# Twelve of sixteen batches rolled into a run-time loop, in two of the four layers of a graph network

## The chip, the core and the metric

The kernel runs on one core of a Trainium2 chip. The metric is the device time of one execution in microseconds. Before the change the median of three runs is 2392.07 us (2391.06 to 2393.24).

## What is computed

The input is x, 16 batches of 1024 nodes with 64 features, and an adjacency matrix of 1024 x 1024. Four attention layers follow each other; each one is added to its input and normed over the features:

```python
x = _layernorm(x + _L0_gnn_ref(x, L0_gnn_W, L0_gnn_a, adj))      # additive attention
x = _layernorm(x + _L1_gnn_ref(x, w0, b0, wa, ba, adj))          # softmax per feature
x = _layernorm(x + _L2_gnn_ref(x, adj, L2_gnn_W, L2_gnn_a))      # additive attention
x = _layernorm(x + _L3_gnn_ref(x, adj, Wh, bh, Wo, bo, g, b))    # dot-product attention
```

The second layer weighs the features of the neighbours, feature by feature:

```python
feat = softplus(x * (INV_SQRT2 * w0) + b0)
scores = feat * wa + ba
attn = softmax(where(mask, scores, -1e9), over neighbours)
out = einsum('bijd,bjd->bid', attn, feat)
```

The fourth layer has four heads and a second attention over their projection. Each attention scores every node against every other, masks, and mixes:

```python
def _gat_layer(h, mask, b):
    scores = einsum('...nd,...md->...nm', h, h)
    attn = softmax(where(mask, scores, NEG), axis=-1)
    return einsum('...nm,...md->...nd', attn, h) + b
h = einsum('bnc,hdc->bhnd', x, Wh)
z = leaky_relu(concatenated heads of _gat_layer(h, mask, bh))
h2 = einsum('bnk,dk->bnd', z, Wo)
z2 = leaky_relu(_gat_layer(h2, mask, bo))      # then layernorm with gamma, beta
```

## The kernel before

x stays in SBUF for all 16 batches (`keep.x`), and so does the mask. The program has a set-up and four stages, one per layer, with a barrier between them. In each stage every engine has its own instruction list, written by hand, and the engines meet only through semaphores that count up over the batches. A wait for "batch b" is a wait for a count such as `HEADS * b + 2`. `wait(engine, semaphore, count)` at L32 emits one, and leaves it out where the count is a number of zero or less.

The order on each engine is the order in which the Python code is run. `additive_layer` (first and third layer) steps over the batches in a Python loop of its own. `feature_layer` (second layer) has a `step(b, s)` for each engine, with `s` the parity of b for the double buffers; each step works on batch b and prepares b + 1 and b + 2. TensorE's step turns the maxima of a tile (L1781), spreads the maximum over the partitions (L1787), sums up the features (L1795) and multiplies mask and weighted features in four banks (L1809, L1813). DVE's step reduces the maximum (L1637, L1640), shifts, splits values into a rounded part and the rest (L1654) and divides. POOL adds the residual (L1592), and DVE takes its sums (L102).

`dot_layer` (fourth layer) cuts a batch into twenty steps: eight for the first head pair ("s0" to "s7"), eight for the second ("r0" to "r7"), and four ("e0" to "e3") for the second attention of the batch before. In each step TensorE computes scores (L1327, L1330, L1333, or L1351 to L1360 for the second attention) into PSUM, ACT takes the exponential (L1175, L1182) into one of four weight buffers, DVE multiplies by the mask (L1027, L1034), and TensorE multiplies with the values (L1375, L1389) one step later. Between scores and product TensorE does the small jobs that the table in `jobs` assigns to the step: the picking of denominators (L1288), the heads (L1295), the projection (L1303) and others. `Before(st)` gives the step whose product follows a step's scores, also over the border of a batch. SP swaps halves of the second attention's operands (L818, L822) and stores a finished batch (L827); it already does so in a run-time loop, `sp.Fori(0, BATCH - 1)`, in both versions.

The change touches the two functions called `run_all`. Before it, each is a Python loop over 16 batches, so that every instruction stands in the program 16 times with its counts as plain numbers:

```python
for b in range(BATCH):
    run_batch(run, b, b % 2, first=b == 0, last=b == BATCH - 1)
```

## Time and profile before

| | us |
|---|---|
| median of three runs | 2392.07 |
| profiled execution, its own time | 2392.07 |
| its span | 2390.3 |
| TensorE (matmul) busy | 2096.2 (88%) |
| DVE busy | 1791.1 (75%) |
| ACT busy | 1321.2 (55%) |
| POOL busy | 720.5 (30%) |

A row of the timeline reads: start in us, duration in us, engine, line, operation, what is written and read, how many records in a row, and in brackets the idle time before it with the engine that ended it. PE is TensorE's matmul, PEld its weight load, SPq the DMA issue of SP. One fp32 matmul call leaves two records of matmul and two of weight load. Register and branch instructions are not shown as rows.

### The profile page before, as it was taken

The numbers are of one execution on the slowest core, as the hardware profiler recorded it, in microseconds if no ns is written. First come the engines' busy times: TensorE is split into PE (matmuls) and PEld (weight loads), VectorE is DVE, ScalarE is ACT, GpSimd is POOL, SyncE is SP. The second block draws the span as 40 slices with busy tenths as digits, with TensorE's granted clock in tenths as the row PEclk, the third lists the DMA queues.
The fourth block names the chain that finished last, engine by engine and source line by source line (L and its number), as shares of the span: only waits on it lengthen the run. The fifth ranks groups of instructions, "written<-read, shape, count | busy, mean of one in ns | idle before, by whom it ended". The sixth has DMA issues, their size and how long they took to land.

```text
span 2390.3 us, 52998 instructions
## 1 busy us (share of the span) xinstructions
PE 2096.2 (88%) x22580; PEld 1379.1 (58%) x22580; DVE 1791.1 (75%) x2182; ACT 1321.2 (55%) x2970; POOL 720.5 (30%) x527
## 2 busy tenths in 40 slices
PE   6888828886788865999999999999999999999993
PEld 5676727776566653555655555555555555654552
DVE  5788838888688875668688788778777778778773
ACT  3576754442376763556466566565566565566552
POOL 1334325665344330003123123123123123123124
PEclk8788969999798986999999999999999999999996
DMA  5000000000000000000000000000000000000000
GB/s 142 2 2 2 2 2 1 1 1 1 2 2 2 3 2 5 1 10 10 5 15 10 6 15 10 6 14 10 6 14 10 6 15 13 2 14 14 2 14 19
DMA packets 30778, 24.69 MB, mean 10 GB/s; under 512 B 21776, under 2 KB 25424, under 8 KB 30544
## 3 DMA queue, kind: packets, MB, share of 16 engines
q1 hardware_dynamic: 30544, 21.31, 3.7%
q8 instruction: 178, 2.92, 0.5%
q14 instruction: 56, 0.46, 0.1%
HBM read 8.72 MB, written 4.19 MB: 5 GB/s over the span
## 4 chain that ended last, share of the span: by engine, by line
PE 58%; DVE 2%; POOL 1%; SPq 0%; ACT 0%; issue 0%; DMA 0%; ACTq 0%; POOLq 0%; DVEq 0%
PE fourth_ps_out L1375 20%; PE fourth_ps_scores L1327 7%; PE fourth_ps_out L1389 5%; PE fourth_ps_scores L1330 5%; PE fourth_ps_scores L1333 5%; PE fourth_ps_prep L1295 3%; PE fourth_ps_prep L1303 3%; PE fourth_ps_prep L1288 3%; PE fourth_ps_scores L1351 2%; PE fourth_ps_scores L1354 1%; PE fourth_ps_scores L1357 1%; PE fourth_ps_scores L1360 1%; PE fourth_ps_prep L1278 1%; PE fourth_ps_prep L1256 1%; DVE fourth_weights L1027 1%; PE fourth_ps_prep L1310 0%
## 5 line engine op out<-in xcount | busy, mean ns | idle before, releaser
L1027 DVE TENSOR_TENSOR fourth_weights<-fourth_weights,keep_mask 128x1024 f32<-128x1024 f32 x512 | 681.3, 1369 | 217.3 <-ACT fourth_weights L1175 215.7
L1175 ACT ACTIVATE fourth_weights<-fourth_ps_scores 128x512 f32<-128x512 f32 x1024 | 529.3, 606 | 422.7 <-PE fourth_ps_scores L1333 422.7
L1375 PE MATMUL fourth_ps_out<-fourth_weights,fourth_x_stage 128*64 128x512 f32 x2048 | 496.5, 605 | 0.0
L1375 PEld LDWEIGHTS fourth_ps_out<-fourth_weights,fourth_x_stage 128*64 128x64 f32 x2048 | 122.9, 136 | 232.6 <-issue 197.5
L1327 PE MATMUL fourth_ps_scores<-fourth_g_high,fourth_x_high 64*128 64x512 f32 x1024 | 230.3, 446 | 2.4 <-DVE fourth_g_low L986 2.4
L1327 PEld LDWEIGHTS fourth_ps_scores<-fourth_g_high,fourth_x_high 64*128 64x128 f32 x1024 | 96.6, 184 | 200.4 <-issue 105.5
L1182 ACT ACTIVATE fourth_weights<-fourth_ps_scores 128x1024 f32<-128x1024 f32 x128 | 125.3, 1025 | 143.0 <-PE fourth_ps_scores L1360 138.0
L634 PE MATMUL first_ps_out<-first_values,first_weights 128*64 128x65 f32 x4096 | 165.3, 244 | 44.0 <-issue 32.1
L1333 PE MATMUL fourth_ps_scores<-fourth_g_low,fourth_x_high 64*128 64x512 f32 x1024 | 203.2, 392 | 0.0
L1330 PE MATMUL fourth_ps_scores<-fourth_g_high,fourth_x_low 64*128 64x512 f32 x1024 | 203.1, 392 | 0.0
L1034 DVE TENSOR_TENSOR fourth_weights<-fourth_weights,keep_mask 128x1024 f32<-128x1024 f32 x128 | 153.0, 1236 | 66.5 <-ACT fourth_weights L1182 66.4
L634 PE MATMUL third_ps_out<-third_values,third_weights 128*64 128x65 f32 x4096 | 162.2, 241 | 44.4 <-issue 32.3
L634 PEld LDWEIGHTS first_ps_out<-first_values,first_weights 128*64 128x64 f32 x4096 | 150.5, 157 | 72.0 <-issue 53.3
L634 PEld LDWEIGHTS third_ps_out<-third_values,third_weights 128*64 128x64 f32 x4096 | 146.6, 153 | 70.8 <-issue 48.7
L431 DVE SCALAR_TENSOR_TENSOR third_weights<-third_row,third_gain,keep_mask 128x1024 f32<-128x1024 f32 x128 | 168.3, 1336 | 10.0 <-ACT third_row L529 9.5
L431 DVE SCALAR_TENSOR_TENSOR first_weights<-first_row,first_gain,keep_mask 128x1024 f32<-128x1024 f32 x128 | 165.7, 1316 | 9.9 <-ACT first_row L529 9.4
L1809 PE MATMUL second_ps_out<-second_parts,keep_mask 128*128 128x256 f32 x1024 | 155.3, 301 | 0.0
L1809 PEld LDWEIGHTS second_ps_out<-second_parts,keep_mask 128*128 128x128 f32 x1024 | 141.1, 204 | 5.6 <-issue 2.7
L1389 PEld LDWEIGHTS fourth_ps_out<-fourth_h_values,fourth_weights 128*64 128x64 f32 x4096 | 124.6, 138 | 18.9 <-issue 17.5
L1389 PE MATMUL fourth_ps_out<-fourth_h_values,fourth_weights 128*64 128x65 f32 x4096 | 133.3, 223 | 1.1 <-DVE fourth_weights L1034 1.1
L881 POOL TENSOR_TENSOR fourth_biased<-fourth_mixed,fourth_rows_in 128x512 f32<-128x512 f32 x16 | 33.1, 2066 | 325.1 <-DVE fourth_mixed L1042 325.1
L1333 PEld LDWEIGHTS fourth_ps_scores<-fourth_g_low,fourth_x_high 64*128 64x128 f32 x1024 | 97.4, 185 | 22.5
(263 smaller groups left out, 3455.4 us busy)
## 6 DMA issues: line engine op xcount, KB each, us to landing
setup_adj<-in_adj SPq DMA_DIRECT2D x8, 512.0 KB, 6.4
fourth_h_high<-fourth_h_high SPq DMA_DIRECT2D x32, 128.0 KB, 2.3
fourth_h_low<-fourth_h_low SPq DMA_DIRECT2D x32, 128.0 KB, 2.3
out<-keep_x SPq DMA_DIRECT2D x16, 256.0 KB, 2.6
keep_x<-in_x SPq DMA_DIRECT2D x1, 512.0 KB, 10.9
fourth_bias_rows<-in_L_gnn_bh SPq DMA_DIRECT2D x8, 0.2 KB
fourth_wh_in<-in_L_gnn_Wh SPq DMA_DIRECT2D x2, 32.0 KB
fourth_wo_in<-in_L_gnn_Wo SPq DMA_DIRECT2D x1, 64.0 KB
```

The source lines that it names most:

```text
L431: dve.scalar_tensor_tensor(out=weights[t % RING][:, :], in0=row[s][:, :], scalar=gain[s][:, t:t + 1], in1=keep.mask[:, t, :].bitcast(F32), ...
L634: last = pe.matmul(ps_out[part, i * WIDE:i * WIDE + AUG], weights[t % RING][:, i * P + c * SIDE:i * P + (c + 1) * SIDE], values[s][:, t, 0 ...
L1027: dve.tensor_tensor(buf[:, :], buf[:, :], keep.mask[:, st.t, :].bitcast(F32), ALU.mult)\
L1034: dve.tensor_tensor(buf[:, :], buf[:, :], keep.mask[:, 2 * p + u, :].bitcast(F32), ALU.mult)\
L1175: act.activation(weights[st.slot + g][:, cols(half)], ps_scores[g][:, cols(half)], ACT.Exp)\
L1182: act.activation(weights[slot + u][:, :], ps_scores[u][:, :], ACT.Exp).then_inc(exp_ready, 2)
L1327: pe.matmul(ps_scores[g][:, cols(half)], x_high[s][rows(g), nodes], g_high[pair][rows(g), cols(half)], start=True, stop=False)
L1330: pe.matmul(ps_scores[g][:, cols(half)], x_low[s][rows(g), nodes], g_high[pair][rows(g), cols(half)], start=False, stop=False)
L1333: last = pe.matmul(ps_scores[g][:, cols(half)], x_high[s][rows(g), nodes], g_low[pair][rows(g), cols(half)], start=False, stop=True)
L1375: last = pe.matmul(ps_out[rows(half), cols(g)], x_stage[st.s][:, st.t, half, :], weights[st.slot + g][:, cols(half)], start=(st.t == 0), s ...
L1389: last = pe.matmul(ps_out[c * SIDE:(c + 1) * SIDE, i * WIDE:i * WIDE + AUG], weights[slot + u][:, i * P + c * SIDE:i * P + (c + 1) * SIDE] ...
L1809: pe.matmul(out, keep.mask[:, t, i * P:(i + 1) * P], parts[s][:, t, :, :].rearrange("p s c -> p (s c)"), start=(t == 0), stop=False, skip_ ...
```

## The change

In the second and the fourth layer the batches are divided anew. In the fourth layer batches 0, 1, 14 and 15 stay written out, and batches 2 to 13 become a run-time loop with six passes of two batches. In the second layer steps 0, 13, 14 and 15 stay written out, and steps 1 to 12 become the loop. Each engine but SP gets a loop of its own; no barrier is added. Inside the loop b is an expression of the loop register, so the counts of waits and the addresses `keep.x[:, b]` are computed at run time.

```diff
-        def run_all(run):
-            for b in range(BATCH):
-                run_batch(run, b, b % 2, first=b == 0, last=b == BATCH - 1)
+        def run_all(engine, run):
+            run_batch(run, 0, 0, first=True)
+            run_batch(run, 1, 1)
+            with engine.Fori(0, (BATCH - 4) // 2) as i:
+                run_batch(run, 2 * i + 2, 0)
+                run_batch(run, 2 * i + 3, 1)
+            run_batch(run, BATCH - 2, 0)
+            run_batch(run, BATCH - 1, 1, last=True)
...
-                run_all(run)
+                run_all(pool, run)
...
-                run_all(run)
+                run_all(dve, run)
...
-                run_all(run)
+                run_all(act, run)
...
-                run_all(run)
+                run_all(pe, run)
...
-        def run_all(step):
...
-            for b in range(BATCH):
+        def run_all(engine, step):
...
+            step(0, 0)
+            with engine.Fori(0, (BATCH - 4) // 2) as i:
+                step(2 * i + 1, 1)
+                step(2 * i + 2, 0)
+            for b in range(BATCH - 3, BATCH):
                 step(b, b % 2)
...
         def has(b):
...
-            return 0 <= b < BATCH
+            return not isinstance(b, int) or 0 <= b < BATCH
...
-                run_all(step)
+                run_all(pool, step)
...
-                run_all(step)
+                run_all(dve, step)
...
-                run_all(step)
+                run_all(act, step)
...
-                run_all(step)
+                run_all(pe, step)
```

How the lists change is seen best at three places. The names in brackets are semaphores that an instruction waits for; a semaphore number that an earlier stage has used is shown under that stage's name (in the fourth layer `first_low_ready` and `first_total_ready` are the ones for the two score operands). ISA and REGISTER_ALU are register instructions of the engine's sequencer.

TensorE, fourth layer, the border between two batches before the change: the last product of the step before, then the scores of the next batch.

```order
L1360 MATMUL fourth_ps_scores<-fourth_h_norm,fourth_ones 128x512 x2
L1389 MATMUL fourth_ps_out<-fourth_h_values,fourth_weights 64x65 [waits fourth_weights_ready]
L1389 MATMUL fourth_ps_out<-fourth_h_values,fourth_weights 64x65 x15
L1389 MATMUL fourth_ps_out<-fourth_h_values,fourth_weights 64x65 [waits fourth_weights_ready]
L1389 MATMUL fourth_ps_out<-fourth_h_values,fourth_weights 64x65 x15
L1327 MATMUL fourth_ps_scores<-fourth_g_high,fourth_x_high 128x512 [waits fourth_exp_ready,first_low_ready,first_total_ready]
L1327 MATMUL fourth_ps_scores<-fourth_g_high,fourth_x_high 128x512
```

The product, two halves of sixteen matmuls, is followed directly by the scores. After the change the end of the loop body on TensorE reads:

```order
L1365 MATMUL fourth_ps_scores<-fourth_h_norm,fourth_ones 128x512 x2
L1391 ISA
L1394 MATMUL fourth_ps_out<-fourth_h_values,fourth_weights 64x65 [waits fourth_weights_ready]
L1394 MATMUL fourth_ps_out<-fourth_h_values,fourth_weights 64x65 x15
L1391 REGISTER_ALU
L1394 MATMUL fourth_ps_out<-fourth_h_values,fourth_weights 64x65 [waits fourth_weights_ready]
L1394 MATMUL fourth_ps_out<-fourth_h_values,fourth_weights 64x65 x15
L794 REGISTER_ALU
L794 COMPARE_AND_BRANCH
```

Between the product and the next scores stand the counter's increment and the branch back. The branch goes to the head of the body, where two register instructions with waits of their own now precede the scores:

```order
L794 UNCONDITIONAL_BRANCH
L794 ISA
L1327 ISA [waits first_total_ready]
L32 ISA [waits first_low_ready]
L1332 MATMUL fourth_ps_scores<-fourth_g_high,fourth_x_high 128x512 [waits fourth_exp_ready]
L1332 MATMUL fourth_ps_scores<-fourth_g_high,fourth_x_high 128x512
```

The two waits moved from the first matmul of the scores to the register instructions ahead of it. ACT, fourth layer, the exponentials of one step before the change:

```order
L1175 ACTIVATE fourth_weights<-fourth_ps_scores 128x512 [waits fourth_weights_used,fourth_scores_full]
L1175 ACTIVATE fourth_weights<-fourth_ps_scores 128x512 [waits fourth_weights_used]
L1175 ACTIVATE fourth_weights<-fourth_ps_scores 128x512 [waits fourth_scores_full]
L1175 ACTIVATE fourth_weights<-fourth_ps_scores 128x512
```

and the same step in the loop:

```order
L1176 ISA
L32 REGISTER_ALU [waits fourth_scores_full]
L1180 ACTIVATE fourth_weights<-fourth_ps_scores 128x512 [waits fourth_weights_used]
L32 REGISTER_ALU
L1180 ACTIVATE fourth_weights<-fourth_ps_scores 128x512 [waits fourth_weights_used]
L1176 REGISTER_ALU
L1180 ACTIVATE fourth_weights<-fourth_ps_scores 128x512 [waits fourth_scores_full]
L1180 ACTIVATE fourth_weights<-fourth_ps_scores 128x512
```

The wait for the scores moved from the first exponential to a register instruction in front of it, and four register instructions stand between the exponentials. The order of the matmuls, exponentials and masks themselves is the same as before everywhere. POOL, second layer, the residual in the loop:

```order
L1600 REGISTER_ALU [waits first_above_ready]
L1601 ISA [waits first_weights_used]
L1601 TENSOR_TENSOR second_norm_y<-second_mixed,keep_x 128x512
L109 TENSOR_TENSOR second_norm_centred<-second_norm_y,second_norm_minus_mean 128x512 [waits setup_loaded2]
```

Both waits of the residual stand on register instructions there; written out, they stand on the TENSOR_TENSOR.

## Rows read from the trace of the kernel before

**Rows 1.** Busy time by stretch: one batch of layer four, layer two, all of layer four.
```profile
core 0: us, PE busy (x) PEld busy (x) DVE busy (x) ACT busy (x) POOL busy (x), PEclk, DMA share, GB/s
1211.55:1300.30 88.75, 88.00 (x743) 49.98 (x743) 68.34 (x69) 51.29 (x91) 22.16 (x15) 1.00 0.04 10
400.00:580.00 180.00, 142.49 (x1091) 131.60 (x1091) 160.74 (x263) 73.55 (x149) 107.37 (x82) 0.91 0.00 1
907.00:2390.30 1483.30, 1419.28 (x11870) 806.86 (x11870) 1096.44 (x1125) 821.79 (x1440) 347.15 (x224) 0.98 0.04 10
```

**Rows 2.** TensorE's waits from 1300 to 1655 us (us in total, times, longest).
```profile
PE fourth_ps_prep L1295 <- DVE fourth_head_recip L991: 3.0, 4, 0.8
```

**Rows 3.** Second layer: its matmuls, waits from 400 to 580 us, two timeline rows.
```profile
L1809 PE MATMUL second_ps_out<-second_parts,keep_mask x1024: 277/281/582, 355.9 to 588.7; 128*128 128x256 f32 x171
...
PE second_ps_wide L1787 <- DVE second_top_wide L1640: 30.5, 12, 2.9
...
DVE second_parts L1654 <- ACT second_parts L1737: 14.5, 12, 1.8
...
494.28 1.26 POOL L1592 TENSOR_TENSOR second_norm_y<-second_mixed,keep_x 128x512 f32<-128x512 f32 x1 [1.94 <-DVE second_mixed L1667]
495.61 0.67 DVE L102 TENSOR_REDUCE second_norm_sums<-second_norm_y 128x8 f32<-128x512 f32 x1
```

**Rows 4.** The page: counts of the engines, instruction queues (packets, MB, share).
```profile
PE 2096.2 (88%) x22580; PEld 1379.1 (58%) x22580; DVE 1791.1 (75%) x2182; ACT 1321.2 (55%) x2970; POOL 720.5 (30%) x527
...
q8 instruction: 178, 2.92, 0.5%
q14 instruction: 56, 0.46, 0.1%
```

**Rows 5.** DMA issues: KB of each, median us from issue to landing.
```profile
first_w<-in_L_gnn_W SPq DMA_DIRECT2D x2, 16.0 KB, 2.0
second_factor_row<-in_L_gnn_wa SPq DMA_DIRECT2D x1, 32.0 KB, 3.2
```

**Rows 6.** Timeline of TensorE at a border between two batches of layer four.
```profile
1257.33 2.09 PE L1389 MATMUL fourth_ps_out<-fourth_h_values,fourth_weights 128*64 128x65 f32 x64
1259.34 0.50 PE L1327 MATMUL fourth_ps_scores<-fourth_g_high,fourth_x_high 64*128 64x512 f32 x2
...
1262.80 2.09 PE L1389 MATMUL fourth_ps_out<-fourth_h_values,fourth_weights 128*64 128x65 f32 x64
```

**Rows 7.** Timeline of DVE, then of ACT, at the same border.
```profile
1257.62 2.36 DVE L1034 TENSOR_TENSOR fourth_weights<-fourth_weights,keep_mask 128x1024 f32<-128x1024 f32 x2 [1.23 <-ACT fourth_weights L1182]
1261.95 1.23 DVE L1027 TENSOR_TENSOR fourth_weights<-fourth_weights,keep_mask 128x1024 f32<-128x1024 f32 x1 [1.98 <-ACT fourth_weights L1175]
1264.93 0.21 DVE L1040 RECIPROCAL fourth_recip<-fourth_ps_out 128x8 f32<-128x8 f32 x1 [1.76 <-PE fourth_ps_out L1389]
...
1260.34 2.06 ACT L1175 ACTIVATE fourth_weights<-fourth_ps_scores 128x512 f32<-128x512 f32 x4 [1.83 <-PE fourth_ps_scores L1333]
```

**Rows 8.** Timeline of POOL and SP: a store in SP's loop, the last one behind it.
```profile
1141.10 1.04 POOL L906 TENSOR_TENSOR keep_x<-fourth_outer_centred,fourth_outer_rstd 128x512 f32<-128x512 f32 x1
1142.35 0.46 SPq L827 DMA_DIRECT2D out<-keep_x  x1
...
2384.71 1.04 POOL L906 TENSOR_TENSOR keep_x<-fourth_outer_centred,fourth_outer_rstd 128x512 f32<-128x512 f32 x1
...
2385.77 0.40 SPq L827 DMA_DIRECT2D out<-keep_x  x1
```

**Rows 9.** Timeline of layer four, 1299 to 1311 us: DVE, TensorE and ACT.
```profile
1299.66 2.33 DVE L1027 TENSOR_TENSOR fourth_weights<-fourth_weights,keep_mask 128x1024 f32<-128x1024 f32 x1
...
1305.68 2.36 DVE L1027 TENSOR_TENSOR fourth_weights<-fourth_weights,keep_mask 128x1024 f32<-128x1024 f32 x2 [0.34 <-ACT fourth_weights L1175]
...
1301.13 2.00 PE L1375 MATMUL fourth_ps_out<-fourth_weights,fourth_x_stage 128*64 128x512 f32 x8
...
1309.12 1.94 PE L1375 MATMUL fourth_ps_out<-fourth_weights,fourth_x_stage 128*64 128x512 f32 x8
...
1308.55 2.06 ACT L1175 ACTIVATE fourth_weights<-fourth_ps_scores 128x512 f32<-128x512 f32 x4 [1.43 <-PE fourth_ps_scores L1333]
```

## The prediction, made before the changed kernel was run

> **What bounds the kernel now.** I read the busy shares by stretch first, then the waits of TensorE, then the timeline at the places that the change touches. The fourth layer takes the largest share of the time: it runs from 907 us to the end, 1483 of 2390.3 us [rows 1]. In its steady part one batch takes 88.75 us and TensorE is busy for 88.00 of them, at the full granted clock [rows 1]. Over four batches TensorE waits for one thing only, DVE's reciprocals of the head sums, 3.0 us in 4 waits [rows 2]. So in this layer time is added exactly when TensorE is made to stand still, and none can be taken away that is not in those 0.75 us per batch. The second layer's main matmuls (L1809) run from 355.9 to 588.7 us [rows 3]. There TensorE is busy for 142.49 of 180 us and DVE for 160.74 [rows 1]; the waits go round from TensorE over DVE and ACT, with 30.5 us of TensorE waiting for the maximum (L1787) in 12 waits, and 14.5 us of DVE waiting for ACT's rounded products [rows 3]. It is bound by a chain over engines in which DVE is almost full, and TensorE has about 2.5 us of slack in each batch. The first and third layers and the set-up are not touched.
>
> **What changes.** No arithmetic, no wait on another engine and no order of work is changed. In both layers twelve of the sixteen batches become six passes through one loop over two batches, on four engines. That adds three things: a branch back, five times per layer and engine; register work that computes each semaphore's target and the addresses of x; and, on some of those register instructions, waits that formerly sat on the matmul or activation itself. It removes instruction traffic: the whole program's was 178 packets on TensorE's queue (2.92 MB, 16.4 KB each) and 56 on the other (0.46 MB, 8.2 KB) [rows 4]. That traffic costs nothing now: in the steady fourth layer no wait of TensorE is left that it could explain [rows 2]. I therefore give its removal 0 us.
>
> **Term A, the branches back of TensorE in the fourth layer.** 22580 matmuls and as many weight loads [rows 4] came in 178 packets, 254 instructions each. One batch has 743 matmuls [rows 1], so the loop body has 2 x 2 x 743 = 2972 of these instructions, 11.7 packets long, beside the register work. Its first packet was fetched 177 us before the branch returns to it. No row shows a jump over such a distance, so I bound it. The fetch of 16 KB should cost what a 16 KB load costs from issue to landing, 2.0 us, or at most what one of 32 KB costs, 3.2 us [rows 5]. I take 2.6. Against that stands what TensorE still has queued when its sequencer meets the branch. The last piece ahead of it is the 64 records of L1389, 2.09 us; right behind it the scores of the next batch (L1327) begin [rows 6]. How many of these are already queued the trace does not say, so the cover is between 0 and 2.0 us; I take half, 1.0. The stall is then 1.6 us, with ends 0 and 3.2, and the term is 5 x 1.6 = 8.0 us, with ends 0 and 16.
>
> The packets show that instructions are brought in pieces of 16.4 and 8.2 KB [rows 4]. The Trainium skill (Runtime: NRT & Kernel Launch, "Instruction fetch mechanics") says that a taken branch whose target is outside the two pages at hand stalls until the page is fetched, and speaks against run-time loops; here it puts the stall at every one of the fourth layer's returns, as I take it, and at those of the second layer too, where it would be 8 us more if nothing hid it. Its page Advanced Engine Details and Errata ("Engine Queue Depths") gives TensorE a queue of 64 instructions; an estimate from that page would cover 64 of the 128 instructions of that 2.09 us piece, 1.0 us. No row here shows either directly.
>
> ACT, DVE and POOL branch back too, with smaller bodies. At this place they have room: DVE has the masks of the last step finished at 1259.98 while TensorE uses them from 1262.80, then idles 1.98 and 1.76 us; ACT idles 1.83 us [rows 7]. A stall of 2.6 us on them fits into the 2.8 us between mask and use, so I add 0.
>
> **Term B, waits that moved onto register instructions.** An instruction that carries its own wait starts at once; a register instruction that carries it makes the sequencer stop, and what follows is sent only afterwards. The SP queue shows the price, since it has a loop already: inside the loop the store of a batch starts 0.21 us after POOL's write of x ends (1141.10 + 1.04 to 1142.35); the last store, behind the loop and with a plain wait, starts 0.02 us after it (2384.71 + 1.04 to 2385.77) [rows 8]. So 0.19 us where the wait is the last to end, and nothing where it has long been met. In ACT's loop body the first exponential of each step now sits behind such a wait. In most steps this is hidden. In ordinary steps the second mask ends 1.0 us or more before its matmul: at 1305.68 DVE's pair takes 2.36 us and TensorE reads it from 1309.12 on [rows 9]. Two places per batch have no such room. One is the first step of the second head pair: DVE's mask runs from 1299.66 for 2.33 us, to 1301.99, inside the 2.00 us of TensorE's L1375 from 1301.13 [rows 9], whose second half needs it. The other is the reciprocal of the head sums, where TensorE waits already [rows 2]. Twelve looped batches x 2 x 0.19 = 4.6 us; ends 0 and, with twice the price at each place, 9.
>
> **Term C, the second layer.** TensorE's body there is 1.4 packets long (12 batches in 180 us are 1091 x 2 instructions, so two batches are 364), so its start may still be at hand; if it is not, 1.6 us of stall falls into the 2.5 us that TensorE waits for DVE in every batch [rows 3]. I cost the returns at 0; without that cover they would be 8 us. POOL's residual stands behind two register instructions with waits, and DVE's sums for the norm follow it; they begin 0.07 us after the residual ends, 494.28 + 1.26 to 495.61 [rows 3]. I add one 0.19 us per looped batch, 2.3 us, with ends 0 and 5.
>
> **Sum.** 8.0 + 4.6 + 2.3 = 14.9 us. The profiled execution took 2392.07 us for a span of 2390.3, 1.8 us around it, and is itself the median of the runs. So 2392.1 + 14.9 = 2407 us, 0.6% slower.
>
> **Rivals.**
> 1. The returns are covered: no more than the queued work is needed to fetch the target, or it is at hand. For it: in the steady part TensorE never waits for instructions [rows 2], so fetching runs well ahead; the piece queued at the return is 2.09 us long, about what the cheaper fetch takes. Against it: a body of 11.7 packets would have to be kept whole, or the whole piece be queued. Then A is 0 and only part of B and C is left: 2392.1 + 3 = 2395 us, no change that can be measured. This is the case on the other side, not slower than before. It decides from the point where fetching takes less than the queued 2.0 us.
> 2. Every step pays. The steady layer has twenty steps in a batch. If the register waits on ACT and TensorE ate the room in all of them, 12 x 20 x 0.19 = 46 us come on top, 2438 plus A, 2446 us. Against it: ACT idles 1.43 us before the exponentials of an ordinary step [rows 9], and a delay of 0.19 fits. A partial form, a third of the steps, is 2415 to 2425 us.
> 3. The returns cost more than one fetch: the next piece is late as well, or DVE and ACT come back so late that TensorE waits again for masks, 2 x 3.2 us per return. Five returns give 32 us, with B and C 39: 2431 us. For it: all four engines branch within one step of each other. Against it: the room in rows 7.
> 4. It becomes faster. The only stock is what the straight-line program loses to its own instruction supply. In the second layer that is part of DVE's and TensorE's small gaps, and 0 in the steady fourth. Twelve batches of the second layer at an assumed 0.25 us each give 3 us, twice that at most: 2386 to 2389 us.
>
> **How the numbers follow.** My forecast, 2399 to 2417 us, has a chance of 0.43; rival 1 has 0.25; rival 2 in its full or partial form 0.14; rival 3 0.13; rival 4 0.05. A difference under 0.2% (4.8 us) can't be told from none. Of rival 1 some 0.20 lies within that bound and 0.05 above it, of rival 4 0.02 within it. Slower by over 0.2% is then 0.43 + 0.05 + 0.14 + 0.13 = 0.75, within 0.22, faster 0.03. The range of 2391 to 2434 us leaves out the full form of rival 2, the top of rival 3 and most of rival 4. The likeliest case alone is 2399 to 2417.
>
> **What would show it.** For A: in the fourth layer five gaps of TensorE of 1 to 3 us ahead of the scores at L1327's successor, one in each second batch between the third and the fourteenth, 2 x 88.75 = 177.5 us plus the gap apart, put down to no other engine; six passes take 6 x 177.5 us plus about 13 us. For B: looped batches take about 0.4 us longer than written-out ones even without a return. For the packets: TensorE's queue still moves about as many as before in time, since the loop is fetched again in each pass; if it moves only about a third, the body was kept and rival 1 holds. For C: the second layer's stretch grows by less than 5 us, and TensorE's wait at the maximum shrinks where a return lies. I am wrong if TensorE's idle time in the steady fourth layer stays at 0.75 us per batch, or if it grows evenly over all steps; and wrong in the sum if the second layer grows by more than 8 us.

## The result and the profile after

The changed kernel takes 2446.69 us (median of 4 runs, 2444.24 to 2451.93), the kernel before 2391.74 us beside it (4 runs, 2391.06 to 2393.24). The ratio is 1.0232, with a 95% interval of 1.0211 to 1.0252: 55 us slower. The forecast was 2407 us with a range to 2434. The direction was right, the size was not, and the time lies outside the range. The profiled execution took 2449.49 us for a span of 2447.7.

The first reading is where the 57.4 us of span went. The view of one line gives the first and last start of a group (count, shortest/middle/longest duration in ns, first to last start in us):

```profile
L634 PE MATMUL third_ps_out<-third_values,third_weights x4096: 219/222/371, 615.7 to 891.3; 128*64 128x65 f32 x196
L1818 PE MATMUL second_ps_out<-second_parts,keep_mask x1024: 277/281/583, 351.8 to 585.0; 128*128 128x256 f32 x171
L1332 PE MATMUL fourth_ps_scores<-fourth_g_high,fourth_x_high x1024: 383/492/793, 934.9 to 2358.1; 64*128 64x512 f32 x171
```

In the kernel before, the rows of the third and the fourth layer read:

```profile
L634 PE MATMUL third_ps_out<-third_values,third_weights x4096: 219/222/371, 619.3 to 885.0; 128*64 128x65 f32 x196
L1327 PE MATMUL fourth_ps_scores<-fourth_g_high,fourth_x_high x1024: 383/492/793, 928.7 to 2301.2; 64*128 64x512 f32 x171
```

The looped second layer takes 233.2 us, before 232.8 [rows 3]. The fourth takes 1423.2 us, and before it took 1372.5: 50.7 us more. The third layer, in which nothing was changed, takes 275.6 us and took 265.7; the first took 4 us less than before. What of these two belongs to the change is a question for the experiments.

Busy time by stretch, with the same columns as [rows 1]:

```profile
400.00:580.00 180.00, 145.24 (x1112) 134.43 (x1113) 160.11 (x261) 73.79 (x148) 108.35 (x82) 0.91 0.00 0
...
1088.90:1177.60 88.70, 87.95 (x743) 49.90 (x741) 68.60 (x68) 51.24 (x90) 22.07 (x14) 1.00 0.05 10
1257.00:1270.10 13.10, 8.81 (x164) 6.97 (x164) 7.30 (x7) 4.82 (x5) 0.00 (x0) 0.93 0.02 5
...
1300.00:1345.00 45.00, 45.00 (x267) 22.70 (x268) 38.16 (x39) 29.90 (x57) 14.06 (x9) 1.00 0.08 18
```

The granted clock is the third number from the end. A looped batch without a return in it (1088.9 to 1177.6) takes 88.70 us, against 88.75 for a written-out one [rows 1]. So the register instructions and the waits on them cost nothing that can be seen. All of the layer's loss is at the five returns. TensorE's waits from 1000 to 2230 us (us in total, times, longest), and its timeline at the first return:

```profile
PE fourth_ps_scores L1332 <- issue: 21.5, 5, 4.5
PE fourth_ps_prep L1300 <- DVE fourth_head_recip L996: 8.1, 13, 0.8
PE fourth_ps_scores L1335 <- issue: 1.3, 3, 0.5
```

```profile
1263.65 2.09 PE L1394 MATMUL fourth_ps_out<-fourth_h_values,fourth_weights 128*64 128x65 f32 x64
1270.03 0.79 PE L1332 MATMUL fourth_ps_scores<-fourth_g_high,fourth_x_high 64*128 64x512 f32 x2 [4.29 <-issue]
```

Five standstills of 4.0 to 4.5 us, with no engine named as releaser: the first matmul after the return has not arrived. The loop's own line shows why (ns, shortest/middle/longest of six; the sixth branch is the one that leaves the loop):

```profile
L794 ACTq COMPARE_BRANCH  x6: 40/45/45, 1264.0 to 2202.1; - x6
...
L794 DVEq COMPARE_BRANCH  x6: 50/56/72, 1265.0 to 2203.2; - x6
L794 PEldq COMPARE_BRANCH  x6: 82/4478/4642, 1265.1 to 2203.2; - x6
```

TensorE's branch takes 4.3 to 4.6 us when it goes back and 0.08 us when it leaves the loop. It is met at 1265.1 us, when only 0.63 us of the last queued piece (to 1265.74) is left. In the 5.1 us from 1265 us on, two packets came over TensorE's instruction queue:

```profile
q8 instruction: 2, 0.03, 4.0%
q14 instruction: 1, 0.01, 0.4%
```

The second part of the loss begins in the gap, 1.7 us before its end (1.5 to 2.2 us before it at the five returns). The granted clock falls to its half level, 1.2 GHz, and stays there when the matmuls go on. Busy time after the first return:

```profile
1268.40:1282.10 13.70, 11.54 (x96) 9.67 (x98) 1.80 (x3) 2.17 (x4) 0.00 (x0) 0.51 0.01 2
1282.10:1296.00 13.90, 13.41 (x80) 6.74 (x76) 11.50 (x13) 7.39 (x14) 4.15 (x2) 1.00 0.01 2
```

The same 13.7 us at half clock come with each of the five returns. In the timeline above, the pair of scores lasts 0.79 us where it lasts 0.50 at full clock [rows 6]. The account for the fourth layer is then 21.5 us of standing and 29.2 us of slow matmuls, 5.8 us per return (1.3 us of the 29.2 are short gaps at L1335 between the slow matmuls). Of the 55 us between the medians, 4 are then outside the fourth layer.

In the second layer TensorE's branch back costs almost nothing:

```profile
L1552 PEldq COMPARE_BRANCH  x6: 76/210/246, 391.5 to 544.3; - x6
```

The body of 1.4 packets is at hand. From 360 to 550 us TensorE's queue moved 2 packets, before 9. Over the whole program it moved 188, before 178 [rows 4]: what the second layer saves, the refetches of the fourth more than use up.

### The profile page after: what moved, and what is told of

It is laid out like the page before. It is cut to its first block, busy times and chain, and to the rows that moved or that the text cites. A ratio compares the mean times of both kernels' runs of the same rounds, so it can differ in the third digit from the quotient of the medians.

```text
span 2447.7 us, 55658 instructions
## 1 busy us (share of the span) xinstructions
PE 2134.4 (87%) x22580; PEld 1408.4 (58%) x22580; DVE 1790.1 (73%) x2182; ACT 1321.1 (54%) x2970; POOL 719.3 (29%) x527
## 4 chain that ended last, share of the span: by engine, by line
PE 58%; DVE 2%; issue 1%; POOL 1%; ACT 0%; SPq 0%; DMA 0%; DVEq 0%; ACTq 0%; POOLq 0%
PE fourth_ps_out L1380 20%; PE fourth_ps_scores L1332 7%; PE fourth_ps_out L1394 5%; PE fourth_ps_scores L1335 5%; PE fourth_ps_scores L1338 5%; PE fourth_ps_prep L1293 3%; PE fourth_ps_prep L1308 3%; PE fourth_ps_prep L1300 3%; PE fourth_ps_scores L1356 2%; PE fourth_ps_scores L1362 1%; PE fourth_ps_scores L1359 1%; PE fourth_ps_scores L1365 1%; PE fourth_ps_prep L1283 1%; DVE fourth_weights L1032 1%; PE fourth_ps_prep L1261 1%
## 5 line engine op out<-in xcount | busy, mean ns | idle before, releaser
L1332 PE MATMUL fourth_ps_scores<-fourth_g_high,fourth_x_high 64*128 64x512 f32 x1024 | 234.3, 453 | 23.8 <-issue 21.5
L1335 PE MATMUL fourth_ps_scores<-fourth_g_high,fourth_x_low 64*128 64x512 f32 x1024 | 209.7, 398 | 1.3 <-issue 1.3
L1338 PE MATMUL fourth_ps_scores<-fourth_g_low,fourth_x_high 64*128 64x512 f32 x1024 | 208.5, 397 | 0.0
L431 DVE SCALAR_TENSOR_TENSOR first_weights<-first_row,first_gain,keep_mask 128x1024 f32<-128x1024 f32 x128 | 164.5, 1307 | 11.1 <-ACT first_row L529 10.8
L1394 PEld LDWEIGHTS fourth_ps_out<-fourth_h_values,fourth_weights 128*64 128x64 f32 x4096 | 132.6, 145 | 18.9 <-issue 17.1
L1394 PE MATMUL fourth_ps_out<-fourth_h_values,fourth_weights 128*64 128x65 f32 x4096 | 141.7, 231 | 1.1 <-DVE fourth_weights L1039 1.1
```

Of the source, the lines that this page charges most:

```text
L431: dve.scalar_tensor_tensor(out=weights[t % RING][:, :], in0=row[s][:, :], scalar=gain[s][:, t:t + 1], in1=keep.mask[:, t, :].bitcast(F32), ...
L1332: pe.matmul(ps_scores[g][:, cols(half)], x_high[s][rows(g), nodes], g_high[pair][rows(g), cols(half)], start=True, stop=False)
L1335: pe.matmul(ps_scores[g][:, cols(half)], x_low[s][rows(g), nodes], g_high[pair][rows(g), cols(half)], start=False, stop=False)
L1338: last = pe.matmul(ps_scores[g][:, cols(half)], x_high[s][rows(g), nodes], g_low[pair][rows(g), cols(half)], start=False, stop=True)
L1394: last = pe.matmul(ps_out[c * SIDE:(c + 1) * SIDE, i * WIDE:i * WIDE + AUG], weights[slot + u][:, i * P + c * SIDE:i * P + (c + 1) * SIDE] ...
```

## Experiments

Each comparison has its own runs of the kernel before, with medians of 2391.03 to 2392.84 us. The fourth layer's length is taken as above, from the first to the last start of the first score group. "Standing" is TensorE's time without a releaser in that layer's loop.

| kernel | ratio (95%) | fourth layer | more than 1372.5 | of it standing | rest |
|---|---|---|---|---|---|
| changed | 1.0232 (1.0211–1.0252) | 1423.2 | 50.7 | 21.5 | 29.2 |
| e1 second only | 1.0025 (1.0008–1.0042) | 1372.4 | 0 | 0 | 0 |
| e2 fourth only | 1.0114 (1.0092–1.0137) | 1401.2 | 28.7 | 16.7 | 12.0 |
| e3 TensorE only | 1.0208 (1.0181–1.0236) | 1423.1 | 50.6 | 21.8 | 28.8 |
| e4 all but TensorE | 1.0033 (1.0015–1.0051) | 1373.6 | 1.1 | 0 | 1.1 |
| e5 two passes | 1.0078 (1.0062–1.0094) | 1382.6 | 10.1 | 3.3 | 6.8 |
| e6 turned | 1.0049 (1.0033–1.0065) | 1377.5 | 5.0 | 2.9 | 2.1 |
| e7 turned, short | 1.0150 (1.0131–1.0168) | 1399.5 | 27.0 | 17.4 | 9.6 |
| e8 pauses | 1.0272 (1.0252–1.0293) | 1435.1 | 62.6 | 40.0 | 22.6 |
| e12 turned, two passes | 0.9990 (0.9973–1.0007) | 1373.8 | 1.3 | 0.2 | 1.1 |

**Which layer: e1 and e2.** One `run_all` is put back in each.

```diff
-            step(0, 0)
-            with engine.Fori(0, (BATCH - 4) // 2) as i:
-                step(2 * i + 1, 1)
-                step(2 * i + 2, 0)
-            for b in range(BATCH - 3, BATCH):
+            for b in range(BATCH):
                 step(b, b % 2)
```

That is e2; e1 does the same to the fourth layer's.

> Only the second layer is looped, the fourth is written out. Theory R (each return of TensorE to a body that is no longer at hand costs 4.5 us of standstill and some 6 us at half clock; a body that is at hand costs nothing): the second layer's return took 0.21 us, so 2392, within 3 us of before. Theory W (register instructions and their waits cost in every looped step): 2392 plus 12 batches x 0.2 to 0.5 us, 2394 to 2398.

> Only the fourth layer is looped, the second is written out. R: all of the loss is here, 2392 + 5 x 10.5 = 2444. W: the same within a few us, so this one only places the loss.

With the second layer alone looped the time is 2399.32 us, with a second layer of 233.0 us and a fourth as before. With the fourth alone it is 2423.31 us, where 2444 was expected. The layer is settled, but e2's returns are cheaper than the changed kernel's:

```profile
L794 PEldq COMPARE_BRANCH  x6: 83/3526/3842, 1269.5 to 2185.4; - x6
```

```profile
1273.40:1285.40 12.00, 11.26 (x114) 7.74 (x116) 6.09 (x7) 5.43 (x10) 4.14 (x2) 0.88 0.01 3
1455.80:1467.80 12.00, 11.26 (x107) 9.49 (x108) 4.26 (x6) 4.13 (x8) 2.41 (x2) 0.72 0.01 3
...
1824.20:1836.20 12.00, 11.25 (x120) 7.38 (x122) 7.35 (x8) 5.33 (x10) 4.14 (x2) 1.00 0.01 3
```

The body is the same, but it lies elsewhere in the program, since the second layer is now written out. The branch takes 3.4 to 3.8 us, with one packet fetched in its time where the changed kernel has two. The standstills of 3.2 to 3.6 us are followed by 6.8, 3.4 or 0 us at half clock instead of 13.7. So the same body costs 10.1 us for each return in the changed kernel and 5.7 here. That its place in the program makes the difference is the likely reading, but it is not the whole of it. The kernel of e5 below has the same instructions ahead of its loop as the changed kernel, and its return has one packet; and of e6's five returns, all of one branch, four have one packet and the last has two. What decides between one and two stays open.

**Which engine: e3 and e4.** In e3 the fourth layer is looped on TensorE alone; in e4 on ACT, DVE and POOL alone.

```diff
         def run_all(engine, run):
+            if engine is not nc.tensor:      # e4: if engine is nc.tensor
+                for b in range(BATCH):
+                    run_batch(run, b, b % 2, first=b == 0, last=b == BATCH - 1)
+                return
             run_batch(run, 0, 0, first=True)
```

> In the fourth layer only TensorE runs a loop; ACT, DVE and POOL have their lists written out (second layer looped as in the changed kernel). R: 2444, all of the loss. W, on ACT and DVE: under 2400. Theory L (the other engines come back late and TensorE waits for them): 2400 to 2415.

> In the fourth layer ACT, DVE and POOL run the loop and TensorE's list is written out (second layer looped). R: 2392 to 2395, no loss. W: 187 register instructions in ACT's body and 104 in DVE's stay, so 2420 to 2446. L: 2410 or more.

TensorE's loop alone gives the whole loss of the layer (2447.60 us, fourth layer 1423.1). The other three engines' loops give 1.1 us in that layer, and TensorE's waits there name only the reciprocal, 9.8 us in 13 waits, as long each as in the kernel before (9.0 us in 12). Their own returns, and the waits on registers on ACT, cost the layer no more than that 1.1 us. The time, 2402.75 us, is above the 2392 to 2395 expected; the rest of it lies outside this layer.

**How many returns: e5.**

```diff
-            with engine.Fori(0, (BATCH - 4) // 2) as i:
-                run_batch(run, 2 * i + 2, 0)
-                run_batch(run, 2 * i + 3, 1)
+            with engine.Fori(0, 2) as i:
+                for k in range((BATCH - 4) // 2):
+                    run_batch(run, 6 * i + 2 + k, k % 2)
```

> As the changed kernel, but the fourth layer's loop takes six batches in a pass: two passes, so one return on each engine instead of five; the second layer's loop stays. All register work and all waits on registers stay in the same twelve batches. Theory R (each return of TensorE in the fourth layer costs about 10.5 us, of which 4.3 are the missing instructions and about 6 the half granted clock after it): the fourth layer grows by 10 us over the 1372.5 of the kernel before, to about 1383, with one gap of 4.0 to 4.6 us and one stretch of 13.7 us at half clock. Theory W (register work and waits moved onto it cost in every batch): the fourth layer stays near 1423. Time by R 2392 + 10 = 2402, and up to 10 more where the first and third layers lie at the longer of their lengths; by W 2440.

The fourth layer takes 1382.6 us where 1383 was expected. One return of 3.50 us, a gap of 3.3 us and 13.7 us at half clock are in it, and twelve batches of register work that cost nothing. The loss goes with the number of returns. The median of the runs is 2410.22 us, though, and the profiled run's 2402.34 the lowest of four; 8 us of that are not in the fourth layer as profiled.

**What is queued ahead: e6 and e7.** TensorE's loop is cut two steps later in the batch (e6), or three (e7); the other engines stay.

```diff
+            if engine is nc.tensor:
+                cut = 2      # e7: 3
...
+                part(2, 0, 0, cut)
+                with engine.Fori(0, (BATCH - 4) // 2) as i:
+                    part(2 * i + 2, 0, cut, STEPS)
+                    part(2 * i + 3, 1, 0, STEPS)
+                    part(2 * i + 4, 0, 0, cut)
+                part(BATCH - 2, 0, cut, STEPS)
+                run_batch(run, BATCH - 1, 1, last=True)
+                return
```

> As the changed kernel, but TensorE's loop in the fourth layer is cut two steps later in the batch: its body runs from the third step of one batch to the second step of the batch after next, so that ahead of the branch stand about 20 records with long ones among them, some 4.7 us of queued work by the records' durations, instead of short ones that last 0.63 us from the branch on. The same instructions in the same order, the same two 16 KB fetches at each return. Theory R (the return costs what its fetch is longer than the queued work, and the granted clock falls only because TensorE stands): the branch still takes 4 to 4.6 us, but the gap of TensorE is 0 to 1 us, no stretch at half clock, and the fourth layer takes 1373 to 1378 us. Rival (the fetch itself or the turn of the program costs, whatever is queued; or the records ahead are not queued since the sequencer waits for another engine there): gaps of 4 us and 1423 remain. A rival in between: cover counts instructions, not their time, then gaps of about 3 to 4 us. Time by R 2392 to 2406, by the rival 2440 to 2450.

> As the one before, but the loop is cut three steps into the batch, where the 20 records ahead of the branch last about 3.3 us. Expected a gap of about 1 us at each return. Theory R1 (the granted clock falls after any standstill): 13.7 us at half clock after each, the fourth layer near 1372.5 + 5 x 7 = 1408. Theory R2 (a standstill of 1 us is too short to lower it): no half clock, and the fourth layer at about 1378.

In e6 the branch back takes 3.3 to 3.9 us in four returns and 4.64 us in the fifth, partly less than the 4 to 4.6 expected (first row, the loop's line), and TensorE works on through it (timeline at the first return):

```profile
L800 PEldq COMPARE_BRANCH  x6: 83/3576/4642, 1274.5 to 2166.7; - x6
```

```profile
1274.15 1.98 PE L1315 MATMUL fourth_ps_prep<-fourth_mixture,fourth_post 128*128 128x512 f32 x4 [0.75 <-DVE fourth_head_recip L1011]
1276.07 1.94 PE L1395 MATMUL fourth_ps_out<-fourth_weights,fourth_x_stage 128*64 128x512 f32 x8
1278.64 0.50 PE L1347 MATMUL fourth_ps_scores<-fourth_g_high,fourth_x_high 64*128 64x512 f32 x2 [0.64 <-issue]
```

The branch is met at 1274.5 us and lasts to 1278.35; the twelve matmuls queued behind it last to 1278.0. What is left is a gap of 0.64 us. The longest of the five is 1.6 us, at the branch of 4.64 us, and none is followed by half clock. The fourth layer grows by 5.0 us instead of 50.7, and the time is 2403.10 us. What covers is the duration of the queued work, not its number of instructions: some twelve long matmuls cover 3.5 us, where some fifteen short ones covered 0.63.

For e7 I expected gaps of 1 us and a fourth layer of 1378 or 1408, and got gaps of 3.1 to 3.9 and 1399.5. The cover was there, but TensorE stood a second time behind the branch (2425.61 us in all):

```profile
1273.69 1.94 PE L1395 MATMUL fourth_ps_out<-fourth_weights,fourth_x_stage 128*64 128x512 f32 x8
1279.05 0.50 PE L1347 MATMUL fourth_ps_scores<-fourth_g_high,fourth_x_high 64*128 64x512 f32 x2 [3.42 <-issue]
```

```profile
L800 PEldq COMPARE_BRANCH  x1: 3410/3410/3410, 1272.4 to 1272.4; - x1
L800 PEldq FUSED_REGOPS  x1: 83/83/83, 1275.9 to 1275.9; - x1
```

The branch is over at 1275.8, when the queued matmuls end at 1275.6. Then TensorE stands 3.4 us more, with the first instructions behind the branch gone through. ACT and DVE have nothing under way from 1277.8 us on, so it isn't they that hold it. Two 16 KB packets came between 1272 and 1279 us, the second, by its record, 0.8 us after the branch had ended. Such a packet comes 0.7 to 1.2 us after the branch in e2 and e6 too, and there TensorE doesn't stand for it. It looks as though the target lay near the end of its piece here, so that the next piece had to be waited for too, without a branch; that is read from one trace and was not tried by itself. As a test of the clock e7 says only that gaps of 3.1 to 3.9 us were followed by 0.78 to 0.89 of the clock over 12 us.

**Standing without a fetch: e8.** Both layers are written out. Ahead of five batches TensorE goes round an empty loop.

```diff
+            pauses = {4: 8, 6: 14, 8: 20, 10: 26, 12: 32}
             for b in range(BATCH):
+                if engine is nc.tensor and b in pauses:
+                    with engine.Fori(0, pauses[b]) as i:
+                        pass
                 run_batch(run, b, b % 2, first=b == 0, last=b == BATCH - 1)
```

> Both layers written out as in the kernel before, but ahead of the batches 4, 6, 8, 10 and 12 of the fourth layer TensorE's sequencer goes 8, 14, 20, 26 and 32 times round an empty loop, of 0.21 us a pass by the second layer's returns: pauses of about 1.7, 2.9, 4.2, 5.5 and 6.7 us, less the 0.6 us that is queued. No instruction is fetched from afar. Theory R: gaps of about 1.1, 2.3, 3.6, 4.9 and 6.1 us; the first two leave the granted clock as it is, the last three are followed by half clock as the returns are, 7 to 14 us of it, and cost 3 to 7 us beyond the gap. Rival (the half clock belongs to the fetch or to the branch from afar, not to the standstill): no half clock at any of the five, and the layer grows only by the sum of the gaps, 18 us. By R it grows by 27 to 40 us.

The line of the empty loops, the first gap, and the stretch after it:

```profile
L795 PEldq COMPARE_BRANCH  x100: 76/208/235, 1256.5 to 2025.0; - x100
```

```profile
1259.34 0.50 PE L1331 MATMUL fourth_ps_scores<-fourth_g_high,fourth_x_high 64*128 64x512 f32 x2 [2.33 <-issue]
```

```profile
1259.80:1270.00 10.20, 10.20 (x96) 9.21 (x94) 2.01 (x3) 2.17 (x4) 0.00 (x0) 0.50 0.01 2
1270.00:1280.00 10.00, 9.65 (x54) 4.33 (x50) 8.10 (x9) 5.61 (x11) 4.15 (x2) 1.00 0.01 2
```

The rival falls: no instruction is fetched from afar, all 95 branches back take about 0.21 us, and the half clock follows all five pauses, for 10.2 us after a gap of 2.33 us and for 13.7 after one of 4.5. A turn took 0.37 us and not 0.21, and 0.62 in the fourth pause, so the gaps came out at 2.3, 4.5, 6.8, 15.2 and 11.1 us; why that pause had slower turns is open. They sum to 40.0 us (2454.23 us in all), and the other 22.6 of the layer's 62.6 us more are slow matmuls. My expectation that the two shortest would leave the clock alone was wrong. Across the runs the length of a standstill alone does not say what follows: 3.15 us was followed by 0 (e2), 3.3 us by 13.7 (e5), 2.33 us by 10.2 (here).

**The rest outside the fourth layer: e9, e10 and e13 to e16.** e1 and e4 were 0.25 to 0.33% slow with a fourth layer within 1.1 us of before, and in the profiles of the changed kernel, e1, e3 and e4 the third layer took 275.6 to 275.9 us. e9 is the kernel before unchanged, e13 is e1 once more. e15 and e16 split e1 by engines as e3 and e4 did, and e10 (from the kernel before) and e14 (from e1) start the third layer later:

```diff
                 pe.wait_ge(keep.first_x_loaded, 16)
+                if stage == "third":
+                    with pe.Fori(0, 5) as i:
+                        pass
```

> The kernel before once more, as a measure of what the comparison itself tells apart and of how long its third layer takes in another execution. Theory N (the third layer's 265.7 or about 276 us is a matter of the execution, not of the program): its third layer may come out anywhere between 265 and 276, and its ratio to itself may lie up to 0.3% from 1. Theory P (it belongs to the program): 265.5 to 266 again, ratio within 0.1% of 1.

> Everything written out as in the kernel before, but ahead of the third layer's first matmul TensorE goes five times round an empty loop, 1.9 us by the 0.37 us of a pass in the run with pauses. No other loop. Theory S (the third layer's length hangs on when it starts: the half clock stretches in it recur every 17.1 us, and what starts later meets more of them): the layer's length changes by more than 2 us from 265.7, up to 276, though its own work is the same. Rival (the length belongs to the second layer's loop, by the instructions that it leaves behind): 265.7 and only the 1.9 us on top, 2394.

> Only the second layer looped, two batches a pass, once more. Theory L (this loop itself makes what follows slower): ratio 1.0025 to 1.003 again and a third layer of about 276 us. Theory N (executions differ, since the stretches at half clock in the first and third layers fall differently, and the first comparison caught such a difference): ratio within 0.2% of 1, the third layer anywhere from 265 to 276.

> As e13, with five turns of an empty loop (1.9 us) ahead of TensorE's first matmul of the third layer. Theory S (the loop shifts where the third layer starts against the recurring stretches at half clock): the third layer leaves 275.9 and takes 266 to 270, the time falls to 2390 to 2394. Theory L: 275.9 stays, 2400.

> Second layer looped on ACT, DVE and POOL alone, TensorE's part written out; the fourth written out. If the rest comes from the waits on registers of those engines at the layer's end or from their code, the third layer is at 276 us and the ratio at 1.0025; if from TensorE's loop, 266 to 270 and a ratio of 1.

> Second layer looped on TensorE alone. The mirror of e15: ratio 1.0025 and a third layer of 276 us if TensorE's loop is the cause, 1 and 266 to 270 if the others' is. By theory N both e15 and e16 lie within 0.2% of 1.

Third layers of 269.6 (e9), 267.7 (e10), 268.6 (e13), 270.2 (e14), 272.2 (e15) and 269.6 us (e16). Ratios of 1.0001 (0.9981–1.0022), 1.0000 (0.9982–1.0018), 1.0009 (0.9996–1.0021), 0.9998 (0.9986–1.0010), 1.0011 (1.0000–1.0023) and 0.9998 (0.9983–1.0013). The same kernel, e1 and e13, has a third layer of 275.9 us in one execution and 268.6 in the other. The unchanged kernel has 265.7 and 269.6. What differs is the granted clock early in the layer. The same 50 us in the changed kernel and in e9, where the kernel before had 1.00:

```profile
630.00:680.00 50.00, 42.71 (x730) 34.41 (x732) 38.94 (x58) 28.42 (x94) 16.95 (x11) 0.76 0.01 2
```

```profile
630.00:680.00 50.00, 41.91 (x856) 34.89 (x858) 42.76 (x59) 26.70 (x86) 18.90 (x13) 0.89 0.01 2
```

So 7 of the third layer's 10 us in the profile can come without any change to the program, as e1 and e13 show. e10 and e14 do not tell whether the layer's start matters: 267.7 lies between the 265.7 and 269.6 of the kernel before, 270.2 between e13's and e1's.

Whether the second layer's loop costs the kernel anything stays open. e1's interval (1.0008–1.0042) and e13's (0.9996–1.0021) overlap. But of the twelve profiled kernels that loop the second layer, on all engines or on some, four have a third layer of 275.6 to 275.9 us, and of the six others none has more than 269.7. And the medians have a pattern that no single profile shows. Take from each kernel's loss what its fourth layer grew by. On the chip of e1 to e8, the six kernels that loop the second layer keep 4.2 to 9.1 us, and the two that write it out (e2 and e8) 1.8 and 0.6 us. On the two other chips, of e9 to e16, the five that loop it keep -1.0 to 1.9 us, and the three others -1.0 to 2.1. So the loop may have cost up to some 9 us on one chip and nothing on two others; no run separates the chip from the program.

**How long a body is kept: e11.** Only the second layer is looped, in two passes of six batches.

```diff
-            with engine.Fori(0, (BATCH - 4) // 2) as i:
-                step(2 * i + 1, 1)
-                step(2 * i + 2, 0)
+            with engine.Fori(0, 2) as i:
+                for k in range(6):
+                    step(6 * i + 1 + k, (1 + k) % 2)
```

> Only the second layer looped, with six batches in a pass and two passes: TensorE's body is 1091 + some 90 instructions, about 4.5 packets of 16 KB, where the changed kernel's is 1.5. One return. Theory K (what is kept is small: a body of 4.5 packets is fetched again): the branch takes 3.4 to 4.6 us as in the fourth layer, part of it hidden by the 2.5 us that TensorE waits in each batch, so 0 to 3 us on the second layer's 233. Rival (bodies of this length are kept, and only the fourth's 12 packets aren't): 0.21 us, as with two batches. Time 2391 to 2403.

```profile
L1547 PEldq COMPARE_BRANCH  x2: 76/156/235, 454.6 to 545.9; - x2
```

The one branch back over 4.5 packets takes 0.235 us (the other record is the one that leaves the loop). My theory K falls: TensorE keeps a body of that length. Between 4.5 packets, kept, and the 11.7 of the fourth layer, not kept, no run lies. Time 2390.51 us, ratio 0.9985 (0.9969–1.0001), no difference that can be told.

**Both remedies: e12.** The fourth layer alone, six batches in a pass on all engines and TensorE's cut as in e6.

```diff
...
+                with engine.Fori(0, 2) as i:
+                    part(6 * i + 2, 0, cut, STEPS)
+                    for k in range(3, 8):
+                        part(6 * i + k, k % 2, 0, STEPS)
+                    part(6 * i + 8, 0, 0, cut)
...
```

> Only the fourth layer looped, in two passes of six batches on all four engines, and TensorE's loop cut two steps later, behind long instructions: one return instead of five, and covered. Theory R: no gap over 1.6 us, no half clock, the fourth layer at 1373 to 1375 us, and a time within 0.2% of the kernel before, 2390 to 2397. If registers or loops cost of themselves, 1380 or more.

```profile
PE fourth_ps_prep L1316 <- DVE fourth_head_recip L1012: 9.0, 12, 0.8
PE fourth_ps_scores L1348 <- issue: 0.2, 1, 0.2
```

The one return takes 3.42 us, and 0.2 us of it are seen. 2391.91 us, ratio 0.9990: a looped fourth layer that costs nothing that can be measured, and no kernel that beats the one before.

## Why the prediction was wrong

**The bound** was read rightly: in the steady fourth layer time is added exactly when TensorE is made to stand [rows 1, 2]. 50.7 of the 55 us are there.

**Term A failed, in its size.** Its step "the fetch of 16 KB should cost what a 16 KB load costs from issue to landing, 2.0 us, or at most what one of 32 KB costs, 3.2 us" [rows 5] set an upper end that was too low: in the changed kernel the branch takes 4.3 to 4.6 us until the next instruction, and over all runs 3.3 to 4.9. With it went "I take half, 1.0" for the cover: it was 0.63 us. Standing is 5 x 4.3 = 21.5 us where 8.0 was forecast and 16 was the end. The larger error is a term that the sum did not have. I let TensorE go on at the old speed after a stall, while each comes with 13.7 us at half clock, 5 x 5.8 = 29 us. The standing alone would have given 2392 + 21.5 = 2414 us, inside the range; it is this missing term that carries the time out of it. That it is the standing and not the fetch is shown from both sides: e8 has standstills without a fetch and the half clock, e6 fetches without a long standstill and no half clock. A hint of it was in the view of stretches, where the granted clock is 1.00 in the steady layer and 0.91 in the second, where TensorE waits [rows 1]. A stall on the engine that sets the time had to be priced with what its clock does next.

The Trainium skill (Runtime: NRT & Kernel Launch, "Instruction fetch mechanics") was right that a taken branch to a far target stalls, and gives no time for it; the runs give 3.3 to 4.9 us. Its window of two pages does not hold here, since a body of 4.5 packets returned in 0.235 us. A body of 1.4 packets, as in the changed second layer, may lie within two pages, so the prediction read the page too strictly where it put a stall there. The same section also states a store of 128 KiB for TensorE, an estimate of eight packets by that page, and the runs agree with that one: 4.5 packets were kept, 11.7 were not.

**Term B** was 4.6 us and is nothing: looped batches take 88.70 us against 88.75. At the reciprocal, one of the two places where the sum put SP's 0.19 us behind a register wait [rows 8], TensorE's wait stayed at 0.75 us in e4, as before. Whether ACT and DVE don't pay that price or hide it the runs don't say. **Term C** was 2.3 us; the second layer grew by 0.4, and what its loop may cost behind it is open. That its returns cost nothing in the layer was right, and by the first reason given: the start was at hand.

**The rivals.** Rival 2 gave 2446 us, almost the time measured, by a mechanism that is not there: the looped batches are not longer. Rival 3, returns that cost more than one fetch, came nearest: two packets fell into each branch, though which of them was the next piece no run shows. At 2431 us it lacked the clock. Rival 1 is false for this kernel but what e12 makes of it: where the queued work is long enough, the return is covered.

**What would show it** pointed at the right rows: five gaps with no releaser, at the place named, a pass apart (187.1 to 188.1 us, where 177.5 and a gap of 1 to 3 were expected). The test on the packets held too: TensorE's queue moved 188 in all, so the fourth's body was fetched again.

## What to carry over

What a run-time loop costs is decided at the branch back, by the length of its body: on TensorE the branch over a body of 4.5 packets of 16 KB took 0.235 us, and over 11.7 packets or more 3.3 to 4.9 us each time. Put the branch behind long instructions that are already released, and make few passes; these two took the fourth layer's loss from 50.7 us to 1.3. Look at the trace after moving the branch: one step further on (e7) the layer still lost 27.0 us. And price a standstill of TensorE with the clock after it: here the slow matmuls cost more than the standing.

## What the runs showed of the hardware

- TensorE's branch back over 11.7 packets or more took 3.3 to 3.9 us with one 16 KB packet in its time, 4.2 to 4.9 with two (e3 has both ends); ACT's, DVE's and POOL's took 0.04 to 0.07 us.
- TensorE's sequencer met the branch 0.63 us before the queued short matmuls ended, and 3.5 us before twelve long ones did (e6).
- Half clock of 10.2 us followed a standstill of 2.33 us, and none followed one of 1.6 (e6) or one of 3.15 (e2).
- A layer of unchanged code took between 265.7 and 275.9 us, with the granted clock over the same 50 us of it between 1.00 and 0.76.
